# First feed-forward group moved into the last full attention rows, its first two hidden blocks into the drain

## The chip, the cores and the metric

The kernel runs on one core of one Trainium2 chip. The metric is the device time of one execution in microseconds. A core has five instruction streams that run side by side and meet at semaphores: PE (TensorE, matrix multiplies), DVE (VectorE), ACT (ScalarE), POOL (GpSimd) and SP (SyncE), which here only issues DMA transfers. A stream executes in order: whatever stands behind a waiting instruction waits too.

## What is computed

A small audio tower. A tokenizer and an attention without weights make 64 rows of 128 tokens by 256 features. Then come two layers of windowed attention and feed-forward; a window of 128 tokens is one of the 64 rows here, so each row is handled alone. Cut to what matters:

```python
def _layer(x, wqkv, qs, ksc, wo, lg, lb, w1, b1, w2, b2):      # twice
    h = shift_token(x)               # second half of the features comes from the token before
    q, k, v = split(h @ wqkv)        # 8 heads of 64
    q, k = l2norm(q) * qs, l2norm(k) * ksc
    q, k = rotary_xpos(q, k)
    o = local_attention(q, k, v)     # causal, in windows; softmax
    x = x + o @ wo
    h = shift_token(x)
    h = (h - mean(h)) / sqrt(var(h) + 1e-05) * lg + lb
    a, g = split(h @ w1 + b1)        # 682 hidden each
    return x + (a * gelu(g)) @ w2 + b2
```

## The kernel before

**Rows and groups.** Attention works on one row (128 tokens) at a time, in a software pipeline; feed-forward works on a group of four rows (512 tokens) at a time, 16 groups a layer. Matrix products are done as three products of a high and a low part, so one hidden block of feed-forward is 12 matmuls of 512 columns (value half and gate half; the tail block has 6). There are six blocks, p = 0 to 5; the third, p = 2, is the tail. The layers follow one another as attention 0, forward 0, attention 1, forward 1.

**Steps.** In attention every stream runs the same function `body` for steps 0 to 68 of a layer. In step t, row t is loaded and transposed, row t-1 is projected to q, k, v and rotated, row t-2 gets its q, k transposes and its scores, row t-3 its softmax (the exponentials `exps` on ACT, `normalise` on DVE) and the transposes of it, row t-4 is weighed with v, row t-5 gets its output product and its sum with the residual (`x_new`, L1219). Steps 0 to 63 are full rows. Steps 64 to 68 are the drain: no new row comes in, and less and less is done. The middle steps are a loop (`run_from`), the first eight and the drain are written out.

**SP's queue.** In step t SP issues: the two halves of row t (L932 128 partitions, L933 shifted by one token, 127 partitions), then the residual of row t-5 (L949, `attn_x_res`), then, once `x_new` of row t-6 is there, its store to `xb` (L952). In steps 64 and 65 it issues the loads of the first and second feed-forward group ahead of the residual (`load_group`: L922 shifted, 127 partitions x 4 rows x 512 B; L923, 128 partitions x 4 rows x 1024 B):

```python
if on(0) and not (layer and step in (0, 1)):
    load_row(sp, layer, t, i, u)
if step in (ROWS, ROWS + 1):
    load_group(sp, layer, layer * GROUPS + step - ROWS, ...)
if on(5):
    sp.dma_start(x_res[:, (u - 5) % 2], xa[t - 5 - L]).then_inc(res_ld[...], 16)
```

**The first group.** Its preparation stands in the drain: statistics (L1155 to L1161) on DVE in step 65, 1/sqrt (L982, `group_rstd`) on POOL at the end of step 65, normalising (L1167, `ffn_xn`) on DVE in step 66, the transposes (`group_turn`, L1319) on PE at the end of step 66, gain, bias and the high part on ACT (L1041, L1046) and the low part on DVE (L1173) in step 67. The first hidden block (p = 0, `hidden`, L1335 to L1337) stands in step 68 ahead of the last row's output product; the second (p = 1) is the first work of feed-forward and waits for `x_new` of row 63. A hidden block p needs the gated product (L1261, DVE) of block p-2. From there on feed-forward is a loop of its own.

**Banks.** The eight PSUM banks are shared: 0, 1 hold q and k before rotation, 2 holds v, 3 and 4 the transposed q and k (and softmax), 5 and 6 the scores, 7 the row's transposes and its output. Feed-forward uses 0, 1 for even blocks, 2, 7 for odd ones, 5, 6 for its transposes, 3, 4 for its output.

On POOL the order in a step of attention is: the rotary sum (L995), 1/norm of k (L1001), its product (L1006), 1/norm of q (L1008), then what else the step holds, `group_rstd` among it.

## Time and profile before

| | us |
|---|---|
| median of 3 runs (lowest to highest) | 2690.91 (2687.47 to 2691.41) |
| the profiled execution, its own time | 2688.39 |
| its span | 2686.6 |
| PE busy in it | 2597.5 (97%) |
| DVE, ACT, POOL busy | 1918.4 (71%), 1702.8 (63%), 1424.5 (53%) |
| layer 0: step 64 begins on PE | 1178.1 |
| layer 0: block p = 3 of the first group begins on PE | 1227.0 |
| layer 1: the same two | 2247.6, 2295.4 |

The profile's page has the busy time of each engine; the views behind it show instructions in order of time (start, duration, engine, line, output <- input; in square brackets the idle time before and what ended it), the chain of work that ended last, and for any stretch the busy time, TensorE's granted clock (PEclk, 1.00 is the upper of two levels, 0.50 the lower) and the share of the core's 16 DMA engines. Matmuls overlap: what one costs in a row of many is the distance of their starts.

### The profile page before, as it was taken

How to read it: one execution, taken by the hardware profiler on the slowest of the kernel's cores; microseconds unless marked ns; L12 is line 12 of the kernel's file. 1: busy time of each engine (PE TensorE's matmuls, PEld its weight loads, DVE VectorE, ACT ScalarE, POOL GpSimd, SP SyncE). 2: the span in 40 equal slices, each digit the busy share in tenths (PEclk: the TensorE clock that was granted, in tenths of full speed). 3: DMA queues.
4: the chain of work that ended last, by engine and by line, in shares of the span. 5: the costliest groups of instructions: out<-in, count | busy, mean ns of one | idle time of the engine just before them, and what ended most of it. 6: DMA issues, size and time to landing. Idle time of an engine off the chain costs nothing.

```text
span 2686.6 us, 71253 instructions
## 1 busy us (share of the span) xinstructions
PE 2597.5 (97%) x25088; PEld 2230.8 (83%) x25088; DVE 1918.4 (71%) x3779; ACT 1702.8 (63%) x4184; POOL 1424.5 (53%) x1512
## 2 busy tenths in 40 slices
PE   7999999889999999988999998999999998999998
PEld 5888888768888888877888887888888887888887
DVE  7777777668878788776555646887788777666664
ACT  4666666557777777774444435777777787444442
POOL 7888888477777776652000006777777664000000
PEclk9999999999999999999999999999999999999999
DMA  2111111111111111121111111111111111222221
GB/s 48 37 48 36 44 36 38 40 43 43 51 38 50 41 37 39 41 67 58 58 53 55 52 34 45 40 48 41 50 38 41 40 36 57 69 82 66 80 73 47
DMA packets 165615, 130.35 MB, mean 49 GB/s; under 512 B 23239, under 2 KB 163689, under 8 KB 165462
## 3 DMA queue, kind: packets, MB, share of 16 engines
q1 hardware_dynamic: 163157, 119.80, 14.5%
q0 software_dynamic: 2304, 8.47, 1.1%
q8 instruction: 100, 1.64, 0.3%
q14 instruction: 54, 0.43, 0.1%
HBM read 77.47 MB, written 50.33 MB: 48 GB/s over the span
## 4 chain that ended last, share of the span: by engine, by line
PE 48%; DVE 21%; ACT 20%; issue 7%; SPq 2%; DMA 1%; DVEq 1%; POOL 0%; ACTq 0%; POOLq 0%
ACT attn_E L1058 15%; PE const_banks L1335 6%; PE const_banks L1336 6%; PE const_banks L1337 6%; DVE attn_neg_top L1231 6%; DVE attn_ss L1224 5%; DVE attn_rot_b L1208 5%; ACT attn_sq L1095 5%; PE const_banks L1473 3%; PE const_banks L1472 3%; PE const_banks L1471 3%; PE const_banks L525 3%; PE const_banks L510 3%; PE const_banks L599 2%; PE const_banks L511 2%
## 5 line engine op out<-in xcount | busy, mean ns | idle before, releaser
L1058 ACT ACTIVATE attn_E<-const_banks,attn_nbias,attn_rn 128x128 f32<-128x128 f32 x1024 | 452.8, 461 | 146.2 <-DVE attn_nbias L1236 146.2
L995 POOL TENSOR_TENSOR attn_qk<-attn_rot_a,attn_rot_b 128x1024 f32<-128x1024 f32 x128 | 303.4, 2370 | 354.1 <-issue 288.6
L982 POOL TENSOR_TENSOR ffn_rstd<-ffn_var,const_neg_half 128x4 f32<-128x4 f32 x32 | 32.3, 1009 | 687.9 <-DVE ffn_var L1161 687.9
L1346 PE MATMUL const_banks<-weights_w_hi,attn_xT_hi 128*128 128x512 f32 x768 | 315.3, 411 | 5.4 <-ACT attn_sq L1095 4.3
L1347 PE MATMUL const_banks<-weights_w_lo,attn_xT_hi 128*128 128x512 f32 x768 | 304.3, 396 | 0.0
L1348 PE MATMUL const_banks<-weights_w_hi,attn_xT_lo 128*128 128x512 f32 x768 | 304.0, 396 | 0.0
L1261 DVE SCALAR_TENSOR_TENSOR ffn_gated<-const_banks,weights_b_col,ffn_gate 128x512 f32<-128x512 f32 (+1 forms) x192 | 143.7, 748 | 216.6 <-ACT ffn_gate L1129 209.7
L1335 PE MATMUL const_banks<-ffn_xT_hi,ffn_w_hi 128*128 128x512 f32 x704 | 283.6, 403 | 6.9 <-DVE ffn_xT_lo L1173 5.4
L1336 PE MATMUL const_banks<-ffn_xT_lo,ffn_w_hi 128*128 128x512 f32 x704 | 280.0, 398 | 0.0
L1337 PE MATMUL const_banks<-ffn_xT_hi,ffn_w_lo 128*128 128x512 f32 x704 | 279.3, 397 | 0.0
L1129 ACT ACTIVATE ffn_gate<-const_banks,weights_b_col 128x512 f32<-128x512 f32 x160 | 110.1, 688 | 228.2 <-PE const_banks L1337 222.7
L1224 DVE TENSOR_REDUCE attn_ss<-attn_sq 128x16 f32<-128x1024 f32 x128 | 156.2, 1220 | 119.6 <-ACT attn_sq L1095 119.6
L1001 POOL TENSOR_TENSOR attn_rn<-attn_ssm,const_neg_half 128x8 f32<-128x8 f32 x128 | 210.9, 1648 | 31.3 <-DVE attn_ssm L1226 29.0
L1058 ACT ACTIVATION_READ_ACCUMULATOR attn_E<-const_banks,attn_nbias,attn_rn 128x1 f32 x1024 | 213.4, 208 | 0.0
L1008 POOL TENSOR_TENSOR attn_rn<-attn_ssm,const_neg_half 128x8 f32<-128x8 f32 x128 | 209.4, 1636 | 0.0
L1201 DVE TENSOR_TENSOR attn_rot_a<-const_banks,weights_cos_s 128x1024 f32<-128x1024 f32 x128 | 156.7, 1225 | 59.2 <-PE const_banks L1348 59.2
L1095 ACT ACTIVATE attn_sq<-const_banks 128x1024 f32<-128x1024 f32 x128 | 131.1, 1025 | 107.0 <-DVE attn_rot_b L1208 107.0
L1139 ACT ACTIVATE ffn_h_hi<-ffn_gated 128x512 fp32r<-128x512 f32 x160 | 101.3, 633 | 140.9 <-DVE ffn_gated L1261 140.9
L1186 DVE TENSOR_TENSOR attn_E<-attn_E,attn_rsum 128x512 f32<-128x512 f32 x256 | 179.6, 702 | 8.8
L1471 PE MATMUL const_banks<-ffn_w_hi,ffn_h_hi 128*128 128x256 f32 x640 | 179.5, 280 | 6.1 <-DVE ffn_h_lo L1269 6.1
L1472 PE MATMUL const_banks<-ffn_w_lo,ffn_h_hi 128*128 128x256 f32 x640 | 179.7, 281 | 0.0
L1473 PE MATMUL const_banks<-ffn_w_hi,ffn_h_lo 128*128 128x256 f32 x640 | 179.5, 280 | 0.0
(179 smaller groups left out, 8009.3 us busy)
## 6 DMA issues: line engine op xcount, KB each, us to landing
attn_x_res<-xa SPq DMA_DIRECT2D x128, 128.0 KB, 4.9
xb<-attn_x_new SPq DMA_DIRECT2D x128, 128.0 KB, 1.7
ffn_x_<-xb SPq DMA_DIRECT2D x32, 512.0 KB
h<-ident_h SPq DMA_DIRECT2D x64, 128.0 KB, 1.7
xa<-ident_n SPq DMA_DIRECT2D x64, 128.0 KB, 1.7
attn_x_<-xa SPq DMA_DIRECT2D x128, 64.0 KB
xa<-ffn_x_new SPq DMA_DIRECT2D x16, 512.0 KB, 3.6
ffn_add<-h SPq DMA_DIRECT2D x16, 512.0 KB, 6.5
```

The lines of the kernel that those rows point to most:

```text
L995: pool.tensor_tensor(qk[:, slot].rearrange("p a n -> p (a n)"), rot_a[:].rearrange("p a h d -> p (a h d)"), rot_b[:].rearrange("p a h d -> ...
L1058: last = act.activation(E[:, r, i], ps_s[:, r, i * P:(i + 1) * P], ACT.Exp, bias=nbias[:, r, i:i + 1], scale=rn[:, slot, h:h + 1], accum_o ...
L1095: act.activation(sq[:].rearrange("p h d -> p (h d)"), ps_qk[:].rearrange("p a n -> p (a n)"), ACT.Square).then_inc(s["squared"], 1)
L1224: dve.tensor_reduce(ss[:], sq[:], AX_X, ALU.add).then_inc(s["normed"], 1)
L1335: pe.matmul(dst, w.w1_hi[:, kk, at], yT_hi[:, slot, kk], start=(kk == 0), stop=False)
L1336: pe.matmul(dst, w.w1_hi[:, kk, at], yT_lo[:, slot, kk], start=False, stop=False)
L1337: last = pe.matmul(dst, w.w1_lo[:, kk, at], yT_hi[:, slot, kk], start=False, stop=(kk == KD - 1))
L1346: pe.matmul(out_, xT_hi[:, slot, k], w.w_hi[:, k, cols], start=(k == 0), stop=False)
L1347: pe.matmul(out_, xT_hi[:, slot, k], w.w_lo[:, k, cols], start=False, stop=False)
L1348: last = pe.matmul(out_, xT_lo[:, slot, k], w.w_hi[:, k, cols], start=False, stop=(k == KD - 1))
L1471: pe.matmul(dst, h_hi[:, slot, k, tok], w.w2_hi[:, k], start=(k == 0), stop=False)
L1472: pe.matmul(dst, h_hi[:, slot, k, tok], w.w2_lo[:, k], start=False, stop=False)
```

## The change

1. The loop of attention on SP and DVE ends four steps earlier; steps 60 to 63 are written out (`tail=4`).
2. SP issues the loads of the first two feed-forward groups in steps 60 and 61 in place of 64 and 65, again between the row's loads and the residual.
3. The first group's statistics stand at the end of DVE's step 62, 1/sqrt at the end of POOL's step 63, normalising at the end of DVE's step 63.
4. `group_turn` of the first group stands at the start of PE's step 65, into banks 3 and 4; the q, k transposes of row 63 behind it wait until ACT has read them. ACT does gain and bias at the start of step 65, the high part behind the copies of q and k; DVE the low part behind `normalise`.
5. Block p = 0 stands at the end of PE's step 65 (banks 0, 1), block p = 1 at the end of step 67 (banks 5, 6). ACT's gelu and DVE's gated product of p = 0 stand in step 67. The wait for `x_new` of row 63 stands at p = 3.
6. In step 66 row 62 is weighed ahead of the transposes of row 63's softmax; ACT's high part of it and the load of the gelu table stand ahead of the copies of row 63's softmax.

```diff
-def run_from(eng, base, count, depth, body, before=None, loop=True):
+def run_from(eng, base, count, depth, body, before=None, loop=True, tail=0):
+    end = count - tail if loop else count
-        with eng.Fori(head // 4, count // 4) as i:
+        with eng.Fori(head // 4, end // 4) as i:
-    for t in range(count, count + depth):
+    for t in range(end, count + depth):
...
+        ps_T_first = banks[:, 3:5]
+        h_first = [banks[:, 5], banks[:, 6]]
...
+        def h_banks(layer, t, p):
+            return h_first if isinstance(t, int) and t == layer * GROUPS + 1 and p == 1 else ps_h[p % 2]
...
-                if step in (ROWS, ROWS + 1):
-                    load_group(sp, layer, layer * GROUPS + step - ROWS, layer * GROUPS // 4, step - ROWS)
+                if step in (ROWS - 4, ROWS - 3):
+                    g = step - ROWS + 4
+                    load_group(sp, layer, layer * GROUPS + g, layer * GROUPS // 4, g)
...
-                if step == ROWS + 1:
+                if step == ROWS - 1:
                     group_rstd(pool, layer * GROUPS)
...
-                if step == ROWS + 3:
-                    group_high(act, layer, layer * GROUPS, 0)
+                if step == ROWS + 1:
+                    group_gains(act, layer, layer * GROUPS)
...
+                if step == ROWS + 1:
+                    group_high(act, layer, layer * GROUPS, 0)
...
+                if step == ROWS + 2:
+                    o_high(act, t - 4)
+                    act.activation(ask[:], c["neg_half"][:, 0:1], ACT.Gelu)
...
+                if step == ROWS + 3:
+                    gate_of(act, layer, layer * GROUPS + 1, 1, 0)
...
                 if step == ROWS + 1:
-                    group_statistics(dve, layer * GROUPS, layer * GROUPS // 4, 0)
+                    group_low(dve, layer * GROUPS, 0)
...
+                if step == ROWS + 3:
+                    block_of(dve, layer, layer * GROUPS + 1, 1, 0)
...
+                if step == ROWS - 2:
+                    group_statistics(dve, layer * GROUPS, layer * GROUPS // 4, 0)
+                if step == ROWS - 1:
+                    group_normalise(dve, layer * GROUPS, 0)
+            run_from(dve, L, ROWS, 5, body, before, tail=4)
...
+            if isinstance(t, int) and t == layer * GROUPS + 1:
+                if p == 1:
+                    pe.wait_ge(s["exp_done"], 2 * ROWS * (layer + 1))
+                if p == 3:
+                    pe.wait_ge(s["x_done"], (layer + 1) * ROWS)
...
+                if step == ROWS + 1:
+                    pe.wait_ge(s["et_done"], 2 * (t - 3))
+                    group_turn(pe, layer * GROUPS)
+                    pe.wait_ge(f["xg"], KD * (layer * GROUPS + 1))
...
+                if step == ROWS + 1:
+                    pe.wait_ge(w.f_split, w.STRIPS * (layer + 1))
+                    pe.wait_ge(s["squared"], L + ROWS)
+                    hidden(pe, layer, layer * GROUPS + 1, 1, 0)
+                if step == ROWS + 3:
+                    hidden(pe, layer, layer * GROUPS + 1, 1, 1)
```

SP behind the loop of attention, before: steps 64 and 65 (L922 and L923 are a group's two loads, L949 the residual, L952 the store).

```order
L922 DMA ffn_x_<-xb 127x4x128
L923 DMA ffn_x_<-xb 128x4x256
L949 DMA attn_x_res<-xa 128x256
L952 DMA xb<-attn_x_new 128x256
L922 DMA ffn_x_<-xb 127x4x128
L923 DMA ffn_x_<-xb 128x4x256
L949 DMA attn_x_res<-xa 128x256
L952 DMA xb<-attn_x_new 128x256
```

SP behind the loop, with the change: steps 60, 61 and the start of 62 (the row's loads are L938 and L939 here, a group's L928 and L929, residual and store L956 and L959).

```order
L938 DMA attn_x_<-xa 128x128
L939 DMA attn_x_<-xa 127x128
L928 DMA ffn_x_<-xb 127x4x128
L929 DMA ffn_x_<-xb 128x4x256
L956 DMA attn_x_res<-xa 128x256
L959 DMA xb<-attn_x_new 128x256
L938 DMA attn_x_<-xa 128x128
L939 DMA attn_x_<-xa 127x128
L928 DMA ffn_x_<-xb 127x4x128
L929 DMA ffn_x_<-xb 128x4x256
L956 DMA attn_x_res<-xa 128x256
L959 DMA xb<-attn_x_new 128x256
```

Both group loads now stand where rows are still being loaded, each ahead of a residual and of the next row.

DVE before, end of step 63 and start of step 64: L1226 closes the norms, L1231 and L1236 make the softmax's bias, L1243 is the low part of a row's weighed values, L1201 the first rotary product of the next row, L1184 and L1186 divide the softmax.

```order
L44 REGISTER_ALU
L1236 TENSOR_TENSOR attn_nbias<-attn_neg_top,attn_rn 128x8
L1243 TENSOR_TENSOR attn_oT_lo<-const_banks,attn_oT_hi 128x512
L634 REGISTER_ALU
L634 COMPARE_AND_BRANCH
L1201 TENSOR_TENSOR attn_rot_a<-const_banks,weights_cos_s 128x1024
L1184 RECIPROCAL attn_rsum<-attn_sums 128x4
L1186 TENSOR_TENSOR attn_E<-attn_E,attn_rsum 128x512
```

DVE with the change, the same place (L1190 is the group's normalising, L1234 the rotary product).

```order
L1264 TENSOR_REDUCE attn_neg_top<-const_banks 128x8
L1269 TENSOR_TENSOR attn_nbias<-attn_neg_top,attn_rn 128x8
L1276 TENSOR_TENSOR attn_oT_lo<-const_banks,attn_oT_hi 128x512
L1190 TENSOR_SCALAR ffn_xn<-ffn_x_,ffn_mv,ffn_rstd 128x256 x4
L1234 TENSOR_TENSOR attn_rot_a<-const_banks,weights_cos_s 128x1024
L1217 RECIPROCAL attn_rsum<-attn_sums 128x4
L1219 TENSOR_TENSOR attn_E<-attn_E,attn_rsum 128x512
```

The normalising, with its wait for POOL, now stands between a row's last operation and the next row's first. The statistics (L1178 to L1184) stand in the same place one step earlier, between L1276 and the next row's low part L1226:

```order
L1276 TENSOR_TENSOR attn_oT_lo<-const_banks,attn_oT_hi 128x512
L1178 BN_STATS ffn_stats<-ffn_x_ 128x6 x4
L49 MEMSET ffn_scratch 128x1
L1182 BN_AGGR ffn_mv<-ffn_stats 128x2 x4
L1184 TENSOR_SCALAR ffn_var<-ffn_mv 128x4
L1226 TENSOR_TENSOR attn_xT_lo<-const_banks,attn_xT_hi 128x256
L1234 TENSOR_TENSOR attn_rot_a<-const_banks,weights_cos_s 128x1024
```

POOL before, the last row's work (step 64) and behind it the 1/sqrt (L982, step 65).

```order
L995 TENSOR_TENSOR attn_qk<-attn_rot_a,attn_rot_b 128x1024
L1001 TENSOR_TENSOR attn_rn<-attn_ssm,const_neg_half 128x8
L1006 TENSOR_TENSOR attn_qk<-attn_qk,attn_rn 128x512
L1008 TENSOR_TENSOR attn_rn<-attn_ssm,const_neg_half 128x8
L982 TENSOR_TENSOR ffn_rstd<-ffn_var,const_neg_half 128x4
```

POOL with the change: row 62's work (step 63), the 1/sqrt (L989), and the start of row 63.

```order
L1008 TENSOR_TENSOR attn_rn<-attn_ssm,const_neg_half 128x8
L1013 TENSOR_TENSOR attn_qk<-attn_qk,attn_rn 128x512
L1015 TENSOR_TENSOR attn_rn<-attn_ssm,const_neg_half 128x8
L989 TENSOR_TENSOR ffn_rstd<-ffn_var,const_neg_half 128x4
L1002 TENSOR_TENSOR attn_qk<-attn_rot_a,attn_rot_b 128x1024
```

The 1/sqrt moved from behind row 63's work to behind row 62's.

## Rows read from the trace of the kernel before

**Rows 1.** The page, part 1: busy time (share of the span) xinstructions.

```profile
PE 2597.5 (97%) x25088; PEld 2230.8 (83%) x25088; DVE 1918.4 (71%) x3779; ACT 1702.8 (63%) x4184; POOL 1424.5 (53%) x1512
```

**Rows 2.** Stretches: busy us and (xcount) by engine, then PEclk, DMA share, GB/s.

```profile
2190.00:2200.00 10.00, 10.00 (x102) 8.48 (x101) 8.05 (x16) 7.98 (x26) 6.67 (x5) 1.00 0.13 38
...
2238.00:2246.00 8.00, 8.00 (x57) 6.87 (x57) 6.72 (x13) 6.16 (x22) 4.77 (x4) 1.00 0.07 21
...
2247.60:2295.30 47.70, 36.18 (x294) 30.68 (x292) 26.02 (x64) 26.21 (x75) 13.22 (x10) 0.89 0.20 61
1178.10:1227.00 48.90, 37.55 (x294) 31.31 (x293) 26.05 (x64) 26.21 (x76) 14.77 (x12) 0.86 0.24 75
```

**Rows 3.** SP in order of time, layer 1: start, duration, line, output<-input.

```profile
2196.70 0.34 SPq L932 DMA_DIRECT2D attn_x_<-xa  x1
...
2236.38 0.27 SPq L922 DMA_DIRECT2D ffn_x_<-xb  x1
2236.70 10.74 SPq L923 DMA_DIRECT2D ffn_x_<-xb  x1
2247.49 0.74 SPq L949 DMA_DIRECT2D attn_x_res<-xa  x1
...
2249.12 13.45 SPq L923 DMA_DIRECT2D ffn_x_<-xb  x1
```

**Rows 4.** The chain that ended last, layer 0: start, duration, what.

```profile
1193.06 5.47 DMA attn_x_res<-xa
```

**Rows 5.** Transfers of the residual, L949, all 128, from issue.

```profile
DMA to landing us min/median/max: 2.2/4.9/5.6
```

**Rows 6.** DVE in order of time, layer 1, steps 60 and 61.

```profile
2215.21 0.41 DVE L1219 TENSOR_TENSOR attn_x_new<-const_banks,attn_x_res 128x256 f32<-128x256 f32 x1
2216.56 1.22 DVE L1224 TENSOR_REDUCE attn_ss<-attn_sq 128x16 f32<-128x1024 f32 x1 [0.93 <-ACT attn_sq L1095]
...
2225.32 0.41 DVE L1219 TENSOR_TENSOR attn_x_new<-const_banks,attn_x_res 128x256 f32<-128x256 f32 x1
```

**Rows 7.** PE in order of time, layer 1: the transposes of rows 61 and 62.

```profile
2217.53 0.44 PE L1359 MATMUL const_banks<-const_ident,attn_x_ 128*128 128x128 f32 x2
...
2227.63 0.44 PE L1359 MATMUL const_banks<-const_ident,attn_x_ 128*128 128x128 f32 x2
```

**Rows 8.** DVE, layer 1, steps 63 to 66.

```profile
2249.48 0.68 DVE L1243 TENSOR_TENSOR attn_oT_lo<-const_banks,attn_oT_hi 128x512 fp32r<-128x512 f32 x1
2250.70 1.23 DVE L1201 TENSOR_TENSOR attn_rot_a<-const_banks,weights_cos_s 128x1024 f32<-128x1024 f32 x1 [0.53 <-PE const_banks L1348]
...
2253.26 0.18 DVE L1184 RECIPROCAL attn_rsum<-attn_sums 128x4 f32<-128x4 f32 x1 [0.53 <-ACT attn_E L1058]
...
2263.74 1.40 DVE L1155 BATCH_NORM_STATS2 ffn_stats<-ffn_x_ 128x6 f32<-128x256 f32 x4
...
2274.75 1.38 DVE L1167 TENSOR_SCALAR ffn_xn<-ffn_x_,ffn_mv,ffn_rstd 128x256 f32<-128x256 f32 x4
```

**Rows 9.** POOL, layer 1, steps 63 and 65.

```profile
2250.87 1.63 POOL L1008 TENSOR_TENSOR attn_rn<-attn_ssm,const_neg_half 128x8 f32<-128x8 f32 x1
...
2265.84 1.01 POOL L982 TENSOR_TENSOR ffn_rstd<-ffn_var,const_neg_half 128x4 f32<-128x4 f32 x1 [3.51 <-DVE ffn_var L1161]
```

**Rows 10.** PE, layer 1, end of the drain and start of feed-forward.

```profile
2280.33 1.09 PE L1431 MATMUL const_banks<-attn_ET,attn_v 128*64 128x128 f32 x16
2284.14 0.76 PE L1335 MATMUL const_banks<-ffn_xT_hi,ffn_w_hi 128*128 128x512 f32 x1 [2.71 <-DVE ffn_xT_lo L1173]
...
2288.58 0.28 PE L1403 MATMUL const_banks<-weights_wo_hi,attn_oT_hi 128*128 128x256 f32 x1
...
2290.76 0.48 PE L1335 MATMUL const_banks<-ffn_xT_hi,ffn_w_hi 128*128 128x512 f32 x1 [0.61 <-DVE attn_x_new L1219]
...
2295.37 0.50 PE L1335 MATMUL const_banks<-ffn_xT_hi,ffn_w_hi 128*128 128x512 f32 x1 [0.17 <-DVE ffn_gated L1261]
```

**Rows 11.** DVE, layer 0, second group normalised.

```profile
1227.93 4.54 DVE L1167 TENSOR_SCALAR ffn_xn<-ffn_x_,ffn_mv,ffn_rstd 128x256 f32<-128x256 f32 x4
```

More of the change, by code:

```diff
@@ L952, in body @@
                     sp.dma_start(xb[t - 6 - L], x_new[:, u % 2]).then_inc(stored[u % 2], 16)
[L954 removed]
+            run_from(sp, L, ROWS, 6, body, before, tail=4)
         def forward_sync(sp, layer):
@@ L1033, in forward_pool, with group_gains @@
             run_from(pool, G, GROUPS, 2, body)
-        def group_high(act, layer, t, u):
+        def group_gains(act, layer, t):
+            src = ps_T if not isinstance(t, int) or t % GROUPS else ps_T_first
             for kk in range(KD):
@@ L1174, in group_low, with block_of @@
                                   ALU.subtract).then_inc(f["xT_lo"], 1)
+        def block_of(dve, layer, t, u, p):
+            k, j = ORDER[p], KH * (t - 1) + p
+            need(dve, f["gate_done"], j + 1)
+            need(dve, f["h_lo"], j - 1)
+            r, at = (P, k) if k < FULL else (HTAIL, TAIL)
+            dve.scalar_tensor_tensor(out=gated[0:r, p % 2], in0=h_banks(layer, t, p)[0][0:r],
+                                     scalar=b1_col[0:r, layer, at:at + 1], in1=gate[0:r, p % 2],
+                                     op0=ALU.add, op1=ALU.mult).then_inc(f["gated_done"], 1)
         def attention_vector(dve, layer, before=None):
@@ L1296, in body @@
                     if on(1):
-                        block_of(t, u, p)
+                        if not (step == 1 and p == 0):
+                            block_of(dve, layer, t, u, p)
                         if p:
@@ L1349, in project, with weigh @@
                 return last
+            def weigh(t, u):
+                b = t - 4
+                need(pe, s["et_done"], 2 * b + 2)
+                need(pe, s["v_done"], min_int(t, L + ROWS))
+                need(pe, s["oT_lo"], b)
+                for j in range(HEADS // 2):
+                    for r in range(2):
+                        h = 2 * j + r
+                        last = pe.matmul(ps_v[r * HD:(r + 1) * HD, j * P:(j + 1) * P],
+                                         v[:, u, h * HD:(h + 1) * HD], ET[:, r, j], start=True, stop=True)
+                last.then_inc(s["o_ps"], 1)
             def body(t, i, u, on):
@@ L1479, in body @@
                 for p in range(KH):
-                    if on(1) and not (step == 1 and p == 0):
+                    if on(1) and not (step == 1 and p < 2):
                         hidden(pe, layer, t, u, p)
```

85 lines of the change are left out of this document (31 added, 54 removed).

## The prediction, made before the changed kernel was run

> **What bounds the kernel now.** I read the page's busy times first: PE 97%, the others 53 to 71% [rows 1]. The table of stretches shows where PE is not full: a full attention row is 10.0 us of PE out of 10.0 at clock 1.00, while the way from step 64 to the first group's block p = 3 holds 36.2 us of PE in 47.7 in layer 1 and 37.6 in 48.9 in layer 0, at a clock of 0.89 and 0.86 [rows 2]. So some 11 us in each layer are to be had in the drain, and anything that holds up a full row costs its whole length, since PE has no slack there. Then I read SP's own timeline and the chain: a group's second load, L923, holds SP for 10.7 and 13.5 us [rows 3], and the residual issued behind it lands 5.5 us after its issue [rows 4], where the median is 4.9 and the least 2.2 [rows 5].
>
> **What a group costs in SP's queue.** While only L922 (127 partitions) is moving, the share of the 16 DMA engines is 0.07 at 21 GB/s [rows 2]: one engine of 16. 508 pieces of 512 B are 260 KB, which is 12 us at 21 GB/s. L923's issue ends 11.1 us after L922's (2236.38 to 2247.44) and the second one's 15.1 us after the first one's (2262.57) [rows 3]; in between stand one group, one residual and one store. A row's shifted half (127 pieces of 512 B) is a quarter of a group's: 3.0 us, with the other half 3.2.
>
> **Part 2 of the change, group loads in steps 60 and 61 (layer 1, by the times of before).** SP loads row 60 at 2196.7 [rows 3], so L928 goes out at 2197.8, behind some 2.7 us of that row. L929's issue ends at 2197.8 + 11.1 + 2.7 = 2211.6. Queued behind it on SP are the residual of row 55, the store of row 54, and row 61.
> - The residual lands at 2211.6 + 5.5 = 2217.1; x_new wants it at 2215.2 [rows 6]. 1.9 us late, 0.9 of it in DVE's idle time behind x_new [rows 6].
> - Row 61 lands some 3.7 us behind the residual, at 2220.8; PE wants it at 2217.5 [rows 7]: 3.3 late.
> - The second L929 ends at 2211.6 + 15.1 + 3.2 = 2229.9, the residual of row 56 lands at 2235.4, where x_new stood at 2225.3 [rows 6], and row 62 at 2239.1, where PE stood at 2227.6 [rows 7]: 11.5 us late in all. The delays don't add up; the last contains the first ones.
> - PE comes back from idle at the lower clock. In before, 12 matmuls after an idle 2.7 us took 4.44 us (2284.14 to 2288.58), and the next 18 took the same 4.4 (2290.76 to 2295.2) [rows 10]; so 1.5 us more.
>
> 13.0 us a layer. Bounds: 10 (a cold start that costs nothing, and 0.75 us less for each group) and 14.5. In before the same loads delayed the drain's x_new only once; that goes, and is in the drain's sum.
>
> **Part 3, the preparation in full rows.** Statistics: 1.4 us and the small operations behind them, 2.0 in all [rows 8], between L1243 and the next low part. DVE idles 0.5 us before the rotary product and 0.5 before the second division [rows 8]: some 1.0 us stays on the path (0.3 to 1.5). Normalising needs the 1/sqrt, and that stands behind all of row 62's work on POOL: L1008 ends at 2252.5 [rows 9], L989 takes 1.0 [rows 9], so it is there at 2253.5. DVE is free for it at 2250.2 [rows 8]. **DVE waits 3.4 us**, then normalises for 1.4 [rows 8]; queued behind are row 63's rotary product, the divisions and the second half of the rotation. The rotary product begins at 2254.9 and not at 2250.7, and with the 0.5 us before the second division [rows 8] 3.6 us stay; PE waits for that softmax and has idled about 3 us, so part of 1.5 us for the clock. I take 4.4 (3.6 to 5.5). In before this wait lay in the drain, off the path.
>
> **Parts 4 to 6, the drain.** I followed the new order with the durations of before. In the tail: behind the weighing of row 63, which ends at 2281.4, before has a wait of 2.7, block p = 0 at the lower clock 4.4, the output product, a wait of 0.6, and p = 1 and p = 2, until p = 3 at 2295.4 [rows 10]: 14.0 us. Now it is p = 1 (2.9), the output product (1.4) and p = 2 (1.5) and then some 1.7 us of waiting for the gated product of p = 1, as DVE does the second group's statistics first: 7.5. That saves 6.5. Ahead of it: no wait for the residual, p = 0 in PE's idle time, statistics and normalising gone; against that, gain and bias delay the exponentials by 0.5 us and the gelu table stands before row 63's copies (0.8). I get the weighing of row 63 4.7 us earlier. Together 11.2 us in layer 1; in layer 0 before is 1.2 us longer over the same way [rows 2], so 12.4. Bounds 9 and 12.5: the low end if block p = 0, which waits on PE for ACT's high part and DVE's low part, holds up the output product behind it.
>
> In layer 0 the second group's normalising takes 4.54 us beside POOL's split of weights, for four operations [rows 11]; three times as long as the four in [rows 8]. It now comes earlier against POOL. Between nothing and 3 us, nearer to nothing as POOL's work comes earlier too: 1.5.
>
> **The sum.** Layer 1: 13.0 + 1.0 + 4.4 - 11.2 = +7.2. Layer 0: 18.4 - 12.4 - 1.5 = +4.5. Together +11.7. Against the profiled execution (2688.4, of which the span is 2686.6) that is 2700.1; the median of the runs shown is 2.5 above it, so **2703** as a median.
>
> **The page on a DMA's speed.** The Trainium skill, page "DMA: Bandwidth & Descriptors", section "Specifications", gives about 27 GiB/s for one engine; by that an estimate of a group's shifted load is 9 us, not 12. The trace has 21 GB/s [rows 2], and it decides.
>
> **Rivals.**
> - *The queue takes the loads without holding rows up*, so that only part 3 is paid: 2690.9 + 2 x 5.4 - 23.6 - 1.5 = 2677; **faster**. It decides if a group passes in less than a row's 10.1 us less 3.2 for the row itself, about 7 us. For it: in before the residual of row 59, issued at 2247.5 behind the first group, was in time. Against: the second was not, 11.1 and 15.1 us are both over 7, and there are rows in between now. 0.15. The same page, section "Why a DMA increments its semaphore by 16 and not by 1", says that on this path 127 partitions go to a single engine while 128 use 16; the share of 0.07 [rows 2] agrees, and by that rule the written-out rows are held up as well.
> - *The stall is about half*, because one engine clears its share faster than the mean of before shows (9 us a group, two groups): 5.5 to 6 us less a layer, 2691. Within the bound. 0.17.
> - *The drain gives little*: p = 0 and the table load lie on the path. At 8 us a layer it is 2690.9 + 36.8 - 16 = 2712. It decides once the low part of the first group is later than the output product that now stands behind block p = 0 in PE's order. 0.16.
> - *The preparation is not done in time*: the group's data land at about 2217 and are used at 2240, so this has no chance worth a number.
>
> **How the numbers follow.** The forecast, 2697 to 2708, has 0.52. From the bounds: 2 x (10 + 0.3 + 3.6 - 12.5) - 3 is about 0, and 2 x (14.5 + 1.5 + 5.5 - 9) = 25, so 2691 to 2716; the low end goes to 2688, as the second rival's 2691 is itself a sum of terms of this size. That leaves out the first rival. A measurement of this kernel can tell about 0.2%, 5.4 us, from no change. Faster by more (under 2685.5) 0.15; within it 0.17; slower (over 2696.3) 0.68.
>
> **What would show it.** In the profile after: SP's L929 ends about 14 us after its L928 in step 60 and the next one 18 us later; DVE waits for a DMA at x_new of row 56, and PE for row 62's data; rows 60 to 62 take some 43 us and not 30. At the end of step 63 DVE waits about 3.4 us for POOL's L989 ahead of L1190. The way from step 64 to p = 3 is near 36.5 us in both layers. If DVE shows no wait for a DMA in steps 60 to 62, the first rival holds; if that way is over 39 us, the third.

## The result, and the profile after

| | before | after |
|---|---|---|
| median of the runs shown, us | 2691.01 | 2703.13 |
| lowest, us | 2687.47 | 2702.10 |
| the profiled execution, us | 2688.39 | 2702.96 |
| its span, us | 2686.6 | 2701.2 |

One of the six runs of the changed kernel took 3185.45 us, at a mean granted clock of 0.75 where the other five had 0.99; the ratio leaves it out, and the median of the five is 2702.96.

The ratio to the kernel before is 1.0049 [1.0037, 1.0062]: slower by half a per cent, 12.1 us between the medians and 14.6 between the two profiled spans. The forecast was 2703.

The page, part 1, of the changed kernel, beside [rows 1]. The busy times did not move; the 14.6 us are idle time of PE.

```profile
PE 2597.1 (96%) x25088; PEld 2231.0 (83%) x25088; DVE 1920.2 (71%) x3779; ACT 1702.8 (63%) x4184; POOL 1423.8 (53%) x1512
```

**Steps 60 and 61 on SP**, layer 1. Columns: start, duration, line, output<-input. This is [rows 3] with the new order; a group's second load is now L929.

```profile
2203.99 0.34 SPq L938 DMA_DIRECT2D attn_x_<-xa  x1
...
2204.76 0.80 SPq L928 DMA_DIRECT2D ffn_x_<-xb  x1
2205.61 13.36 SPq L929 DMA_DIRECT2D ffn_x_<-xb  x1
2219.02 0.74 SPq L956 DMA_DIRECT2D attn_x_res<-xa  x1
...
2220.33 0.38 SPq L938 DMA_DIRECT2D attn_x_<-xa  x1
...
2221.21 3.53 SPq L928 DMA_DIRECT2D ffn_x_<-xb  x1
2224.79 12.65 SPq L929 DMA_DIRECT2D ffn_x_<-xb  x1
2237.49 0.75 SPq L956 DMA_DIRECT2D attn_x_res<-xa  x1
```

L929 holds SP for 13.36 and 12.65 us. Its issue ends 15.0 us after row 60's load went out (2203.99 to 2218.97), and the second one's 18.5 us later. Behind the first stand the residual (2219.02) and row 61 (2220.33), and behind the second the next residual.

**What PE and DVE make of it.** PE's transposes of rows 61 and 62, which answer to [rows 7], and DVE's x_new in layer 1, which answers to [rows 6]; in square brackets the idle time ahead of an instruction and what ended it. The first two rows are from layer 1, the next two the same transposes in layer 0.

```profile
2228.26 0.44 PE L1401 MATMUL const_banks<-const_ident,attn_x_ 128*128 128x128 f32 x2 [2.91 <-DMA attn_x_<-xa]
...
2246.81 0.69 PE L1401 MATMUL const_banks<-const_ident,attn_x_ 128*128 128x128 f32 x2 [8.61 <-DMA attn_x_<-xa]
...
1151.18 0.44 PE L1401 MATMUL const_banks<-const_ident,attn_x_ 128*128 128x128 f32 x2 [2.72 <-DMA attn_x_<-xa]
...
1169.66 0.69 PE L1401 MATMUL const_banks<-const_ident,attn_x_ 128*128 128x128 f32 x2 [7.04 <-DMA attn_x_<-xa]
```

```profile
2243.03 0.42 DVE L1252 TENSOR_TENSOR attn_x_new<-const_banks,attn_x_res 128x256 f32<-128x256 f32 x1 [7.44 <-issue]
```

In layer 1 PE idles 2.91 and 8.61 us for the rows' data, and row 62's transposes take 0.69 us and not 0.44, at a granted clock of 0.50. The whole of row 62 ran at 0.82. Row 61, behind the shorter wait, ran at 1.00. From row 60's transposes to step 64 it is 53.1 us in layer 1 (2215.28 to 2268.42) and 53.8 in layer 0, where the kernel before takes 40.1 in both. VectorE's x_new comes after 7.44 us of idle time (its releaser is given as "issue": a wait that the view can't name; the residual behind the second load, issued at 2237.49, is what it reads; in the first experiment below the view names it).

**Step 63.** DVE's normalising of the first group, and what follows on PE.

```profile
2274.90 1.38 DVE L1190 TENSOR_SCALAR ffn_xn<-ffn_x_,ffn_mv,ffn_rstd 128x256 f32<-128x256 f32 x4 [3.51 <-POOL ffn_rstd L989]
```

```profile
2278.37 1.94 PE L1460 MATMUL const_banks<-const_ident,attn_E 128*128 128x128 f32 x8 [2.95 <-DVE attn_E L1219]
2280.24 1.74 PE L1389 MATMUL const_banks<-attn_ET,attn_v 128*64 128x128 f32 x16
```

DVE waits 3.51 us for the 1/sqrt on POOL. PE then idles 2.95, and its next 8 and 16 matmuls take 1.94 and 1.74 us, at a granted clock of 0.55; the same 16 take 1.09 in a full row.

**The way from step 64 to block p = 3**, in the table of stretches (busy us of PE, PEld, DVE, ACT and POOL, then PEclk, DMA share, GB/s), and p = 3 itself. This answers to the last two lines of [rows 2].

```profile
2268.40:2309.90 41.50, 33.55 (x294) 27.69 (x292) 24.74 (x54) 26.36 (x76) 13.45 (x10) 0.96 0.10 30
1192.10:1234.10 42.00, 33.75 (x296) 27.65 (x292) 25.40 (x54) 26.51 (x76) 14.07 (x11) 0.96 0.15 49
```

```profile
2309.95 0.50 PE L1365 MATMUL const_banks<-ffn_xT_hi,ffn_w_hi 128*128 128x512 f32 x1 [1.72 <-DVE ffn_gated L1205]
```

41.5 and 42.0 us, where the kernel before takes 47.7 and 48.9; the clock is 0.96 and not 0.89 and 0.86. Together: +13.0 and -6.2 in layer 1, +13.7 and -6.9 in layer 0.

### The profile page after: what moved, and what is told of

Same layout as the page of the kernel before. It is cut to its first block and busy times, and to the rows that moved or that the text cites. A ratio compares the mean times of both kernels' runs of the same rounds, so it can differ in the third digit from the quotient of the medians.

```text
span 2701.2 us, 71143 instructions
## 1 busy us (share of the span) xinstructions
PE 2597.1 (96%) x25088; PEld 2231.0 (83%) x25088; DVE 1920.2 (71%) x3779; ACT 1702.8 (63%) x4184; POOL 1423.8 (53%) x1512
## 5 line engine op out<-in xcount | busy, mean ns | idle before, releaser
L989 POOL TENSOR_TENSOR ffn_rstd<-ffn_var,const_neg_half 128x4 f32<-128x4 f32 x32 | 32.3, 1009 | 669.6 <-DVE ffn_var L1184 669.6
L1234 DVE TENSOR_TENSOR attn_rot_a<-const_banks,weights_cos_s 128x1024 f32<-128x1024 f32 x128 | 156.7, 1224 | 71.3 <-PE const_banks L1378 71.3
```

## The experiments

Each kernel ran on the chip with the kernel before; the ratio is to that, with its 95% interval. "Way" is the time on PE from the first projection of step 64 to the first matmul of block p = 3, layer 0 and layer 1; "rows" is the time from row 60's transposes to step 64. "Both" is the cut load with the early 1/sqrt; "late weights", "p = 1 back" and "rows cut too" each add one edit to it, "early statistics" adds one to "late weights", and "DVE written out" one to that.

| run | median, us | ratio | rows | way |
|---|---|---|---|---|
| before | 2689.0 to 2691.0 | 1 | 40.1, 40.1 | 48.9, 47.8 |
| after | 2703.1 | 1.0049 [1.0037, 1.0062] | 53.8, 53.1 | 42.0, 41.5 |
| loads only | 2708.8 | 1.0074 [1.0057, 1.0091] | 53.1, 53.0 | 45.5, 45.5 |
| cut 112 + 15 | 2676.0 | 0.9950 [0.9933, 0.9967] | 39.7, 39.7 | 42.0, 42.0 |
| early 1/sqrt | 2697.5 | 1.0028 [1.0016, 1.0041] | 53.7, 52.8 | 38.6, 37.8 |
| both | 2669.1 | 0.9928 [0.9911, 0.9944] | 39.8, 39.7 | 38.7, 37.9 |
| before, cut | 2687.7 | 0.9991 [0.9981, 1.0000] | 40.1, 40.1 | 47.5, 45.6 |
| late weights | 2666.9 | 0.9918 [0.9901, 0.9934] | 39.7, 39.7 | 38.8, 38.8 |
| p = 1 back | 2671.5 | 0.9932 [0.9915, 0.9949] | 39.7, 39.7 | 38.6, 37.8 |
| cut 113 + 14 | 2697.6 | 1.0028 [1.0017, 1.0039] | 50.5, 49.8 | 41.6, 42.8 |
| loads apart | 2689.4 | 0.9997 [0.9987, 1.0006] | 44.0, 41.9 | 42.0, 42.0 |
| rows cut too | 2669.0 | 0.9922 [0.9905, 0.9938] | 39.7, 39.6 | 38.8, 37.9 |
| early statistics | 2662.1 | 0.9896 [0.9880, 0.9913] | 39.7, 39.7 | 36.8, 36.0 |
| DVE written out | 2654.5 | 0.9873 [0.9856, 0.9889] | 39.5, 39.7 | 36.7, 36.9 |

### Is it the loads? The kernel before with its loads in steps 60 and 61

```diff
-                if step in (ROWS, ROWS + 1):
-                    load_group(sp, layer, layer * GROUPS + step - ROWS, layer * GROUPS // 4, step - ROWS)
+                if step in (ROWS - 4, ROWS - 3):
+                    g = step - ROWS + 4
+                    load_group(sp, layer, layer * GROUPS + g, layer * GROUPS // 4, g)
...
-            run_from(sp, L, ROWS, 6, body, before)
+            run_from(sp, L, ROWS, 6, body, before, tail=4)
```

> The kernel before with one part of the change alone: the two group loads go out on SP in steps 60 and 61, everything else of the preparation stays where it was. Theory (the shifted part of a group's load holds up what is queued behind it in the full rows): rows 60 to 62 take 13.0 us longer in layer 1 and 13.7 in layer 0, as in the changed kernel; against that the drain loses its wait for the residual (2.4 us on VectorE in each layer, 2.5 to 3 on PE). Sum +26.7 - 5 = +22, so about 2713 us. Rival (the stall in the changed kernel comes from the added work on VectorE or from the order of PE, not from the loads): no stall in steps 60 to 62, the drain's wait for the residual is gone, 2686 us.

Measured: 2708.8 us, 19.7 over the kernel before. The second load of each group on SP in layer 1 (L924 is L923 of the kernel before), PE's transposes of rows 61 and 62, DVE's x_new in step 61, and the two ways:

```profile
2207.57 12.68 SPq L924 DMA_DIRECT2D ffn_x_<-xb  x1
...
2226.13 12.65 SPq L924 DMA_DIRECT2D ffn_x_<-xb  x1
```

```profile
2229.60 0.69 PE L1361 MATMUL const_banks<-const_ident,attn_x_ 128*128 128x128 f32 x2 [2.37 <-DMA attn_x_<-xa]
...
2248.12 0.69 PE L1361 MATMUL const_banks<-const_ident,attn_x_ 128*128 128x128 f32 x2 [7.21 <-DMA attn_x_<-xa]
```

```profile
2244.27 0.42 DVE L1221 TENSOR_TENSOR attn_x_new<-const_banks,attn_x_res 128x256 f32<-128x256 f32 x1 [5.93 <-DMA attn_x_res<-xa]
```

```profile
2270.00:2315.50 45.50, 33.42 (x296) 28.16 (x292) 26.00 (x64) 26.27 (x75) 13.21 (x10) 0.96 0.09 27
1191.00:1236.50 45.50, 33.52 (x295) 28.19 (x292) 26.02 (x64) 26.27 (x75) 14.71 (x12) 0.96 0.13 44
```

The stall is there without any of the added work: 13.0 and 12.8 us. The rival falls, and the view names the residual as what x_new waits for. The drain gives back 3.4 and 2.2 us, where no group load stands ahead of the residual any more: 25.8 - 5.6 = 20.2, and 19.7 was measured. So moving the loads alone costs 20 us, and the rest of the change earned 6 to 8 of it back (2708.8 against 2703.1; 19.7 against 12.1, each to the kernel before that ran beside it).

### Is it the one engine? The shifted load cut into 112 and 15 partitions

```diff
-            sp.dma_start(y[1:P, u, :, 0:P], shifted(xb, local)).then_inc(y_ld[u], 16)
+            sp.dma_start(y[1:113, u, :, 0:P], shifted(xb, local)[0:112]).then_inc(y_ld[u], 16)
+            sp.dma_start(y[113:P, u, :, 0:P], shifted(xb, local)[112:P - 1]).then_inc(y_ld[u], 16)
...
-            need(dve, y_ld[u], 32 * (i + 1))
+            need(dve, y_ld[u], 48 * (i + 1))
```

> The changed kernel, with the shifted part of a group's load cut into 112 and 15 partitions instead of 127; the same bytes, the same place. Theory (127 partitions go to one of the 16 DMA engines, 112 to 16 and 15 to 15, so the share of a group on the busiest engine falls from 508 packets of 512 B to 32): the stall in steps 60 to 62 goes, 13.0 and 13.7 us, so 2703 - 27 = 2676 us, and SP's L929 ends about 2 us after it was issued and not 13. Rival (the bytes or the number of packets hold up SP's queue, whatever the engine): 2703 us, as the changed kernel.

Measured: 2676.0 us. SP in step 61 of layer 1; L928 and L929 are the two pieces, L930 is the unshifted load:

```profile
2201.91 0.84 SPq L928 DMA_DIRECT2D ffn_x_<-xb  x1
2202.80 0.74 SPq L929 DMA_DIRECT2D ffn_x_<-xb  x1
2203.57 0.39 SPq L930 DMA_DIRECT2D ffn_x_<-xb  x1
```

The load behind the shifted pieces holds SP for 0.39 us and not 13, with the same bytes. Both stalls are gone: the rows take 39.7 us. The table of stretches shows what the DMA engines do meanwhile, first in the changed kernel while L929 holds SP, then with the cut for 3 us from L930's issue on (the last two numbers are the share of the 16 engines and GB/s):

```profile
2207.00:2215.00 8.00, 8.00 (x91) 6.97 (x91) 6.25 (x12) 6.80 (x22) 4.94 (x4) 1.00 0.07 21
```

```profile
2203.60:2206.60 3.00, 3.00 (x15) 2.43 (x13) 2.30 (x5) 2.05 (x9) 2.92 (x3) 1.00 0.84 233
```

A share of 0.07 is 1.1 of 16 engines: only the shifted load moves, and what stands behind it in SP's queue isn't under way. With the cut the unshifted load moves too and the share is 0.84. So the 27 us are the price of a load that keeps about one of the sixteen engines busy and holds back the rest of the queue.

The same edit on the kernel before changes little:

> The kernel before, with the shifted part of a group's load in 112 and 15 partitions and nothing else changed. It measures what the cut brings without the change, so that the changed kernel with the cut can be compared with it. Theory (in the drain of the kernel before the residual waits behind a group's load, 2.4 us on VectorE; the kernel with the loads alone moved had a way from step 64 to p = 3 of 45.5 us in both layers against 48.9 and 47.8): both ways shorten to about 45.5, so 2689 - 5.6 = 2683 us. Rival (the wait for the residual is hidden by the next one): 2689 us.

Measured: 2687.7 us, 2.7 less, half of what I expected; the interval of the ratio ends at 1.0000.

```profile
2246.10:2291.60 45.50, 33.41 (x294) 28.10 (x292) 26.01 (x64) 26.20 (x75) 13.21 (x10) 0.96 0.19 57
1177.90:1225.40 47.50, 36.44 (x296) 30.37 (x292) 26.09 (x64) 26.28 (x75) 14.80 (x12) 0.89 0.23 72
```

The way in layer 1 is 2.2 us shorter, as with the loads moved. In layer 0 it is 1.4 and not 3.4 shorter: the clock over it is 0.89 and not 0.96. PE's wait ahead of block p = 0 is 2.71 us in both layers; over the 4.3 us behind it the clock is 0.66 in layer 0 and 1.00 in layer 1. Why the two differ is not shown. The expectation took layer 0's 45.5 from the run with the loads moved, where the stretch ran at 0.96. This run also says what the rest of the change is worth with the loads out of its way: 2676.0 against 2687.7, 11.7 us, and 18.6 us with the early 1/sqrt (2669.1, below) added.

### Two sizes that differ by one: 113 and 14

The changed kernel again; the number of pieces and their bytes are nearly those of the cut into 112 and 15.

```diff
-            sp.dma_start(y[1:P, u, :, 0:P], shifted(xb, local)).then_inc(y_ld[u], 16)
+            sp.dma_start(y[1:114, u, :, 0:P], shifted(xb, local)[0:113]).then_inc(y_ld[u], 16)
+            sp.dma_start(y[114:P, u, :, 0:P], shifted(xb, local)[113:P - 1]).then_inc(y_ld[u], 16)
```

> The changed kernel, with the shifted part of a group's load cut into 113 and 14 partitions instead of 112 and 15; nothing else differs from the run with that cut (2676 us). Theory (the number of engines is the largest divisor up to 16 of the number of partitions, so that 113, a prime, is on one engine and 14 on 14): a group's longest share falls from 508 to 456 packets, 1.3 us at 24 ns a packet, and each of the stalls stays but for 2.6 us a layer: 2703 - 5 = 2698 us. Rival (cutting the transfer in two is what helps, whatever the sizes): 2676 us.

Measured: 2697.6 us. SP in step 60; L929 is the piece of 14 partitions.

```profile
2201.50 11.91 SPq L929 DMA_DIRECT2D ffn_x_<-xb  x1
```

L929 holds SP for 11.9 us behind the piece of 113, and from 2203 to 2212 us the share of the engines is 0.07 at 21 GB/s, as with 127. It is not the cutting that helps; 112 partitions spread and 113 don't. The Trainium skill, page "DMA: Bandwidth & Descriptors", section "Why a DMA increments its semaphore by 16 and not by 1", gives the rule: a DMA uses the largest number of engines up to 16 that divides the size of the slowest dimension on both sides. By it 112 gets 16, 15 gets 15, 14 gets 14, and 113 and 127, both primes, get one. The three runs agree with it: with the cut at 112 the share rises to 0.84, with the cut at 113 and with the whole load it stays at 0.07, and they take 2676.0, 2697.6 and 2703.1 us. The stall shrank from 13.7 and 13.0 us to 10.4 and 9.7, by 3.3 in each layer, where the piece is 11% shorter; I had expected 2.6.

### Does the second load cost more because of the first? Loads in steps 56 and 60

```diff
-                if step in (ROWS - 4, ROWS - 3):
-                    g = step - ROWS + 4
+                if step in (ROWS - 8, ROWS - 4):
+                    g = (step - ROWS + 8) // 4
...
-            run_from(sp, L, ROWS, 6, body, before, tail=4)
+            run_from(sp, L, ROWS, 6, body, before, tail=8)
```

> The changed kernel, uncut loads, with the two group loads in steps 56 and 60 and not 60 and 61. Theory (each load holds up SP's queue by itself; the second stall was 8.5 us because it stood on the first one's 2.9 and left no time to catch up): four rows apart each costs what the first one did, about 3 us and 1.5 for the clock, 9 us a layer and not 13.0 and 13.7: 2703 - 9 = 2694 us. Rival (the stall is a sum of 12 us of transfer each, less a fixed slack): 2703 us. Another (one group alone is hidden): 2682 us.

Measured: 2689.4 us, 13.7 less than the changed kernel. PE's waits for rows' data over the end of layer 1 (total, times, longest):

```profile
PE const_banks L1401 <- DMA attn_x_<-xa: 4.7, 2, 2.5
```

Four rows apart each load costs PE 2.2 to 2.8 us of waiting. From the transposes of the row before to those of the row that waits it is 2.3 to 2.9 us longer than the usual 10.0. In two of the four cases the row behind the wait then takes 11.4 us at a clock of 0.85; in the other two it takes 9.86 at 1.00. The other rows take 9.81 to 9.97 us, where eight rows of the kernel before take 10.03 on average. Over steps 56 to 64 the excess is 6.2 us in layer 0 and 5.4 in layer 1, where I expected 9. So the second load in a row costs more because of the first: 2.9 us of waiting and then 8.6, against 2.2 to 2.8 each time.

### The 1/sqrt at the head of POOL's step 63

```diff
+                if step == ROWS - 1:
+                    group_rstd(pool, layer * GROUPS)
                 if on(1):
                     b, slot = t - 1, (u - 1) % 2
...
-                if step == ROWS - 1:
-                    group_rstd(pool, layer * GROUPS)
```

> The changed kernel, with the 1/sqrt of the first group at the head of GpSimd's step 63 and not at its end; the loads as they are. Theory (VectorE's 3.5 us wait for it at the end of step 63 lies on the path and costs 4.4 us in each layer with the clock): the wait goes, 2703 - 9 = 2694 us. Rival (the wait hides another one: the softmax of row 63 is late for the sums or the rotated rows anyway): the wait moves to the next instruction and the time falls by less than 3 us.

> Both edits on the changed kernel: the shifted load in 112 and 15 partitions, and the early 1/sqrt. If the two costs are independent: 2703 - 27 - 9 = 2667 us, 0.9% under the kernel before. If each covered part of the other (the stall gave GpSimd and VectorE time), between 2667 and 2676 us.

Measured: 2697.5 us, 5.6 less than the changed kernel; on top of the cut load 2669.1, 6.9 less than 2676.0. DVE's normalising and PE's next wait, in the first of the two, layer 1:

```profile
2265.54 2.11 DVE L1190 TENSOR_SCALAR ffn_xn<-ffn_x_,ffn_mv,ffn_rstd 128x256 f32<-128x256 f32 x4
```

```profile
2277.08 1.06 PE L1434 MATMUL const_banks<-const_ident,attn_qk 128*128 128x128 f32 x8 [2.29 <-issue]
```

DVE no longer waits, but the four operations take 2.11 us and not 1.38, as POOL now works beside them, and 2.29 us of idle time stand ahead of PE's transposes of row 63's q and k, where the changed kernel had 1.45 for gain and bias there and 1.27 further on. These transposes read POOL's product, which ends at 2276.98, 0.1 us before they start:

```profile
2275.94 1.04 POOL L1015 TENSOR_TENSOR attn_qk<-attn_qk,attn_rn 128x512 f32<-128x512 f32 x1
```

By the medians the edit is worth 2.8 and 3.5 us a layer, by the ways 3.3 to 4.2; the forecast was 4.4. With the cut load:

```profile
2235.60:2273.40 37.80, 32.26 (x294) 26.45 (x292) 25.22 (x54) 26.23 (x76) 12.50 (x9) 1.00 0.13 39
1176.30:1215.00 38.70, 33.55 (x294) 27.99 (x292) 25.27 (x54) 26.26 (x76) 13.09 (x10) 0.96 0.18 58
```

The ways are 37.8 and 38.7 us, at a clock of 1.00 and 0.96. The two costs add: the cut alone gives 27.1 us and the 1/sqrt alone 5.6, 32.7 together, and both in one kernel give 34.0 (2703.1 to 2669.1).

### Block p = 1 back in the forward part

```diff
-                if step == ROWS + 3:
-                    hidden(pe, layer, layer * GROUPS + 1, 1, 1)
...
-                    if on(1) and not (step == 1 and p < 2):
+                    if on(1) and not (step == 1 and p == 0):
```

> The changed kernel with the cut load and the early 1/sqrt (2669 us), with block p = 1 of the first group back in the forward part, behind the output product of row 63, and block p = 0 left in the drain. Theory (PE idles 2.3 us for the low part of row 63's values when p = 1 is not there, and the wait of 1.7 us ahead of p = 3 takes up part of the shift): 1.5 us a layer, 2672 us. Rival (the whole block of 2.9 us goes onto the path in each layer): 2675 us. A third (the wait ahead of p = 3 takes up all of it): 2669 us.

Measured: 2671.5 us against 2669.1. The way is the same as with p = 1 in the drain, 37.8 and 38.6 us. PE's output product of row 63 and block p = 3, layer 1:

```profile
2269.05 0.35 PE L1447 MATMUL const_banks<-weights_wo_hi,attn_oT_hi 128*128 128x256 f32 x1 [1.47 <-ACT attn_oT_hi L1062]
...
2275.05 0.50 PE L1366 MATMUL const_banks<-ffn_xT_hi,ffn_w_hi 128*128 128x512 f32 x1 [0.16 <-DVE ffn_gated L1206]
```

With p = 1 gone from its place PE idles 1.47 us for row 63's values, and the wait ahead of p = 3 is 0.16 and not 1.7. The third answer was right for the stretch in question: the wait ahead of p = 3 takes up the whole block. The 2.4 us between the medians don't show on the way; the two traces differ by 2.1 us before row 63 of layer 0, where the kernels are the same, so I don't read them as the price of the block. The banks of q, k and the scores for p = 1 bring nothing as the change stands.

### The second group: statistics and weights

Three further edits, each on top of the one before. First, POOL's splits of the next layer's weights one step later in layer 0 (and the third right behind the second):

```diff
-                if layer < LAST and step is not None and step <= w.PIECES:
-                    if step == 1:
+                if layer < LAST and step in (0, 2, 3):
+                    if step == 2:
                         pool.wait_ge(s["out_ps"], (layer + 1) * ROWS)
                     if step:
-                        w.split_attention(pool, layer + 1, step - 1)
-                    if step < w.PIECES:
-                        w.load_attention(pool, layer + 1, step)
+                        w.split_attention(pool, layer + 1, step - 2)
+                    w.load_attention(pool, layer + 1, step - 1 if step else 0)
+                    if step == 3:
+                        w.split_attention(pool, layer + 1, 2)
```

> The changed kernel with the cut load and the early 1/sqrt (2669 us), and in layer 0's forward part GpSimd's three splits of the next layer's weights in steps 2, 3 and 3 and not 1, 2 and 3, so that none runs beside VectorE's normalising of the second group. Theory (the four operations take 5.7 us beside GpSimd's work and 1.4 alone, and PE waits 3.2 us for them and then runs at the lower clock): 2669 - 4 = 2665 us. Rival (the collision moves to the third group and costs there what it cost at the second): 2669 us.

Measured: 2666.9 us. DVE's normalising of the second group in layer 0; in the changed kernel it is this row, with PE's wait for it behind it:

```profile
1234.60 5.74 DVE L1190 TENSOR_SCALAR ffn_xn<-ffn_x_,ffn_mv,ffn_rstd 128x256 f32<-128x256 f32 x4
```

```profile
1240.39 1.87 PE L1346 MATMUL const_banks<-const_ident,ffn_xn 128*128 128x128 f32 x8 [3.19 <-DVE ffn_xn L1190]
```

and now it is

```profile
1215.71 1.38 DVE L1192 TENSOR_SCALAR ffn_xn<-ffn_x_,ffn_mv,ffn_rstd 128x256 f32<-128x256 f32 x4
```

5.74 us against 1.38, and PE's 3.19 us are gone. The third group's four operations now take 5.78, beside the split that was moved, and PE doesn't wait for them. In layer 0 the second group's transposes start 2.9 us behind block p = 3 and not 6.2, and take 1.04 us and not 1.93; the way in layer 1, where nothing was changed, is 0.9 longer. The medians differ by 2.2 us where 4 was expected, the profiled spans by 5.2. The Trainium skill, page "SBUF — State Buffer", section "Who interferes with whom", says that VectorE's tensor_scalar in a mode with two ports and GpSimd's operations hold one port pair in turn; the longer duration beside GpSimd's work agrees, but no run here tells the port from another cause.

Second, on top of that, the second group's statistics on DVE at the end of step 67, ahead of x_new of row 63:

```diff
+                if step == ROWS + 3:
+                    group_statistics(dve, layer * GROUPS + 1, layer * GROUPS // 4, 1)
...
-                        if p == 0:
+                        if p == 0 and step != 1:
                             group_statistics(dve, t, i, u)
```

> The kernel with the cut load, the early 1/sqrt and the weight splits a step later (2667 us), and the second group's statistics on VectorE ahead of x_new of row 63, where VectorE idles 3.1 us, and not between it and the gated product of p = 1. Theory (PE's wait of 1.7 us ahead of p = 3 in each layer comes from the 2.0 us of these statistics): 1.7 us a layer, 2667 - 3 = 2664 us. Rival (the gated product waits for the gelu anyway): 2667 us.

Measured: 2662.1 us, 4.8 less, where 3 was expected; the ways are 2.0 and 2.8 shorter. The last matmul of p = 2 and the first of p = 3 in layer 1, 0.23 us apart and with no idle time in brackets between them:

```profile
2266.31 0.39 PE L1371 MATMUL const_banks<-ffn_xT_hi,ffn_w_lo 128*128 128x512 f32 x1
2266.54 0.45 PE L1369 MATMUL const_banks<-ffn_xT_hi,ffn_w_hi 128*128 128x512 f32 x1
```

Third, DVE's attention loop ends 20 rows before the last and not 4, so 16 more rows a layer are written out:

```diff
-            run_from(dve, L, ROWS, 5, body, before, tail=4)
+            run_from(dve, L, ROWS, 5, body, before, tail=20)
```

> The kernel with early statistics, and VectorE's attention loop ends 20 rows before the last and not 4: 16 more rows in each layer are written out, with the same operations in the same order. Rows 62 and 63, written out, took 9.86 us where a row of the loop takes 10.03. Theory (the loop's register work between VectorE's instructions lies on the path, some 0.16 us a row): 32 x 0.16 = 5 us less than the kernel with early statistics. Rival (the two rows are short because of where they stand, next to the drain): no difference.

Measured: 2654.5 us, 7.6 less. PE's transposes four rows apart in the same part of layer 1, first with DVE in its loop, then written out:

```profile
2090.53 0.44 PE L1405 MATMUL const_banks<-const_ident,attn_x_ 128*128 128x128 f32 x2
...
2130.73 0.44 PE L1405 MATMUL const_banks<-const_ident,attn_x_ 128*128 128x128 f32 x2
```

```profile
2095.38 0.44 PE L1405 MATMUL const_banks<-const_ident,attn_x_ 128*128 128x128 f32 x2
...
2134.93 0.44 PE L1405 MATMUL const_banks<-const_ident,attn_x_ 128*128 128x128 f32 x2
```

40.20 us for four rows against 39.55. The 16 rows of each layer that are now written out take 3.2 us less in layer 0 (160.8 and 157.6) and 2.5 in layer 1 (160.8 and 158.2): 5.7 of the 7.6 us, 0.16 to 0.2 us a row. The rest is outside these rows and not explained. DVE's waits point to where the 5.7 come from: between the maximum of the scores (L1266) and the bias made from it (L1271), in total, times and longest, in the loop and written out:

```profile
DVE attn_nbias L1271 <- DVE attn_neg_top L1266: 20.3, 104, 0.2
```

```profile
DVE attn_nbias L1271 <- DVE attn_neg_top L1266: 14.1, 72, 0.2
```

In a row of the loop DVE idles 0.2 us between the two, where the trace has a register operation of the wait; in a row written out, the second follows at once. There are 32 such gaps fewer, 6.2 us. That this operation is the cause is read from these rows and was not tried by itself; that writing the rows out saves the time is measured. From 2090 to 2190 us PE is given as busy for 99.92 and 100.00 of 100 us in the two kernels, so its busy share did not show the loss; the number of its matmuls in that stretch does, 997 and 1011.

### A transfer off the path

The kernel with the cut load and the early 1/sqrt, and the rows' loads cut too:

```diff
-            sp.dma_start(x[1:P, u % 2, P:D], row[0:P - 1, P:D]).then_inc(x_ld[u % 2], 16)
+            sp.dma_start(x[1:113, u % 2, P:D], row[0:112, P:D]).then_inc(x_ld[u % 2], 16)
+            sp.dma_start(x[113:P, u % 2, P:D], row[112:P - 1, P:D]).then_inc(x_ld[u % 2], 16)
...
-                    need(pe, x_ld[u % 2], 32 * (2 * i + u // 2 + 1))
+                    need(pe, x_ld[u % 2], 48 * (2 * i + u // 2 + 1))
```

> The changed kernel with the cut group load and the early 1/sqrt (2669 us), and the shifted half of every attention row's load cut in the same way, 112 and 15 partitions. In full rows that transfer of some 3 us is behind 10 us of PE, and PE shows no wait for it. Theory (a transfer off the path gains nothing from being faster): 2669 us, within 2. Rival (it shares its engine with residual and store, and a row is held up by them a little each time): some 0.1 us a row, 2656 us. Another (one more DMA issue a row on SP delays what is behind it): slower than 2671 us.

Measured: 2669.0 us, against 2669.1. The residual's transfer, from issue to landing, without and with the rows cut (KB, then the median in us):

```profile
attn_x_res<-xa SPq DMA_DIRECT2D x128, 128.0 KB, 4.9
```

```profile
attn_x_res<-xa SPq DMA_DIRECT2D x128, 128.0 KB, 2.0
```

It lands in 2.0 us and not in 4.9, and the time is the same: in full rows nothing on the path waits for these transfers.

## Why the prediction was right, and where it wasn't

The terms, profiled execution against profiled execution, in us:

| term | forecast | layer 0 | layer 1 |
|---|---|---|---|
| stall in steps 60 to 62, and the statistics | +13.0 and +1.0 | +13.7 | +13.0 |
| DVE's wait and the drain | +4.4 and -12.4; +4.4 and -11.2 | -6.9 | -6.2 |
| behind p = 3 in layer 0 | -1.5 | +0.7 | |
| up to row 60 of layer 0 | 0 | +0.4 | |

The sum is 14.6 where 11.7 was forecast. That the median of 2703.1 met the forecast to 0.1 us is partly luck: I added 2.5 us for the distance of the profiled execution of before from its median, and the changed kernel's profiled execution is at its median. Within the sum the misses partly cancel: 2.2 us too low behind p = 3, 0.7 too low for layer 0's stall and 1.7 for the drains, against 2.0 too high for the statistics.

**The stall** was right, and so was its working: L929 ended 18.5 us after the first one (18.3), PE's idle time in layer 1 was 2.91 + 8.61 = 11.52 (11.5), the clock cost the rest of 13.04 (1.5), all of it behind the second wait; rows 60 to 62 took 43.2 us (43). In layer 0 nearly the same total is made up otherwise: 2.72 + 7.04 = 9.76 us of idle time and some 3.9 for the clock, 0.83 over the first 9.8 us of row 61 and 0.76 over row 62. So what the clock adds was right for one layer and too small for the other. The experiments show the mechanism that the prediction only argued: it is the loads, and it is that they keep one engine busy. The first rival ("without holding rows up") and the second ("about half") fall with them.

**The statistics** cost nothing that shows, and the 1.0 was wrong: with the loads cut, the same rows take 39.7 us with the statistics in them and 40.1 in the kernel before, less by about what two rows written out save (2 x 0.17).

**DVE's wait** was 3.51 us (3.4), but its price was put too high: removing it gave 2.8 to 3.5 us a layer by the medians (3.3 to 4.2 by the ways), not 4.4. PE then idles 2.3 us ahead of the transposes of row 63's q and k, until POOL's product is there.

**The drain.** The tail was right: from the end of the weighing of row 63 to p = 3 it is 7.6 us (7.5), with the wait of 1.72 us (1.7) ahead of p = 3. Ahead of it the gain was put too high: with DVE's wait removed the way is 9.9 us shorter in layer 1 and 10.2 in layer 0, where I had 11.2 and 12.4. It is inside the bounds of 9 to 12.5. The mark that I gave for it was wrong: I wrote that the way would be near 36.5, and over 39 if the third rival held. DVE's wait at the end of step 63 falls on PE behind the start of step 64, so my own terms make it 36.5 + 4.4 = 40.9. It was 41.5 and 42.0. By the mark as written the third rival would hold, and it doesn't: in layer 1 the low part ends at 2291.65 and block p = 0 starts at 2292.60 with no idle time ahead of it, and without DVE's wait the ways are 37.8 and 38.7.

**Layer 0's normalising** went the other way: the four operations took 5.74 us where before they took 4.54 [rows 11], as all of them now fall beside POOL's work, and PE waits 3.19 us for them. In the kernel before it waited 2.46:

```profile
1232.53 1.72 PE L1319 MATMUL const_banks<-const_ident,ffn_xn 128*128 128x128 f32 x8 [2.46 <-DVE ffn_xn L1167]
```

The difference of 0.73 us is the +0.7 of the table. I had expected 1.5 us of gain. The order of the two engines gave no number for that overlap, and the bounds (0 to 3 us of gain) left out a loss.

**One sentence of the ground was too strong**: that a full row has no slack because PE is busy for all of it. Writing DVE's rows out takes 0.16 to 0.2 us off each.

## What to carry to other kernels

Before a transfer is moved, look at how many engines it uses and what stands behind it in its queue: a load of 127 partitions ran on about one engine (share 0.07), held SP for 13 us, and made a change cost 12 us that with two pieces of 112 and 15 gains 11.7. When an early step needs a result of a second engine, move that engine's part too, to where its inputs are there. And set the price of a wait by what is late next, not by its length.

## What the hardware showed that I had not expected

- The number of partitions decides: 112 + 15 gave 2676.0 us, 113 + 14 gave 2697.6, 127 gave 2703.1, with the same bytes; the share of the DMA engines rose to 0.84 in the first and stayed at 0.07 in the other two.
- Two such loads a step apart cost PE 11.5 us of waiting; four steps apart, 2.2 to 2.8 each.
- The length of a wait did not settle the clock behind it: after waits of 2.70 and 2.91 us for a row's data PE ran on at 1.00, after waits of 2.50 and 2.82 the row ran at 0.85.
- A PE that the profile shows busy for 10.0 of 10.0 us still lost 0.16 to 0.2 us a row to VectorE's loop: 5.7 us for 32 rows written out.
- One normalising of four rows takes 1.38, 2.11 or 5.74 us on VectorE, by what GpSimd does beside it.
- The kernel with the cut load, the early 1/sqrt, the late weights, the early statistics and DVE's rows written out (2654.5 us, 0.9873 [0.9856, 0.9889]) is faster than both the kernel before and the changed one; the longest idle time left in its drain is 2.3 us a layer on PE, ahead of row 63's q and k.
